# Issuing the transfers of the row maxima from ScalarE instead of the sync queue in a two-layer attention kernel

## The chip, the cores and the metric

One NeuronCore of a Trainium2 chip runs the whole program. The metric is the device time of one execution in microseconds; the program before takes 1774.21 us in the median of three runs. The engines are TensorE (PE, with its weight loads as PEld), VectorE (DVE), ScalarE (ACT), GpSimd (POOL) and the sync engine (SP), which here only issues DMAs.

## The reference

For 8 batches of 512 tokens with 256 channels, two transformer layers are computed. Layer 0 has a causal self-attention and a cross-attention (16 heads of 16 channels each, their outputs added), a projection and a quantized feed-forward net. Layer 1 has a cross-attention and a feed-forward net that is quantized with one scale over all tokens, so its feed-forward runs as a tail when all batches are through. Cut to what matters here:

```python
att = jnp.einsum('bhqd,bhkd->bhqk', q, k) * scale
att = jnp.where(causal[None, None], att, -jnp.inf)
y = jnp.einsum('bhqk,bhkd->bhqd', jax.nn.softmax(att, axis=-1), v)
```

The softmax is what the change touches: the kernel subtracts the maximum of each query's row before it takes the exponential.

## The kernel before, in words

**Units.** An attention unit is `(batch, p, g)`: p is `s` (self-attention of layer 0, causal), `x` (cross-attention of layer 0) or `f` (cross-attention of layer 1), and g one of four groups of four heads. There are 96 units, in the order `ORDER` (line 84). A regular turn of the steady part holds twelve: x0 to x3 and s0 to s3 of one batch and f0 to f3 of the batch before. The text calls them by these names.

**Maxima.** While unit u runs, TensorE also computes the scores of a later unit for their maxima alone (`maxima`, line 1579), and VectorE reduces each bank to a column of negated maxima (line 1372). For the unit after u, POOL then splits the maxima into two float16 parts (`negmax`, line 936, lines 941 to 945), TensorE turns them into rows (`negmax_T`, line 1603, line 1607), ScalarE copies the rows from PSUM to `nrow` (line 1042; the copy itself is line 1007), and two DMAs of 4 KB put them into two more rows of `stack`, next to the queries (line 770, line 774). The final scores of the unit (`scores`, line 1610, line 1619) multiply 50 rows instead of 48, so that the maximum is subtracted within the matmul. The first of them waits for both transfers (line 1615).

**Scores, exponentials, values.** A unit has 16 banks of scores: four blocks j of keys times four heads c. They go through a ring of three PSUM banks: the scores of bank k wait until ScalarE has taken the exponential of bank k-3 (line 1053 is the exponential). Behind the last two heads of a block, TensorE multiplies the probabilities of the block before with the values (`values`, line 1625, line 1633).

**Order.** One list of steps, written out ahead of the run, is walked by every engine, and each takes from it what it has to do (`walk`, line 385). Within a unit (`unit_slot`, line 130), `negmax_T` of the next unit comes after the first two scores of block 2. ScalarE thus does two exponentials of block 2, the copy to `nrow`, whatever other work was dealt to that place, and the other two exponentials. Between them lies the other work of the batch: projections (line 1563, copied by ScalarE at line 1039, split by POOL at 932 and 934, stored by SP at 746), norms, the feed-forward net with its GELU and quantization (ScalarE lines 1075, 1082 and 1088, POOL line 965), and the output projection.

**The sync queue.** SP walks the same list in order and does what it meets: it loads the tokens (734), stores the parts of the projected queries and keys (746), loads them regrouped into `stack` (767, eight DMAs for a unit), stores results (779, 780), and, in `negmax_T`, waits until ScalarE's copy is done and then issues the two transfers. What stands behind such a wait in the list waits too, and `negmax_T` itself stands behind what came before it.

Of the kernel before, what the change touches and what calls it, by code (L numbers as in the profile page):

```python
# [40 lines left out]
NT = T // P  # L41
# [6 lines left out]
PARTS = 2  # L48
ROWS = 3 * D
AUG = ROWS + PARTS  # L50
HALF = P // 2
PAIRS = HU // 2
# [11 lines left out]
STACKS = 4  # L64
# [320 lines left out]
def walk(eng, steps_of):  # L385

    for keys in TURNS:
        for key in keys:
            if key[0] in steps_of:
                steps_of[key[0]](Step(key, None))  # L390
# [4 lines left out]
def two_layers_kernel(nc, x, ctx_512, L0_xattn_Wk, L0_xattn_bk, L0_xattn_Wq, L0_xattn_bq, L0_xattn_Wv, L0_xattn_bv,  # L395
# [4 lines left out]
    with ExitStack() as ctx:  # L400
# [6 lines left out]
        def sem(name):  # L407
            return ctx.enter_context(nc.semaphore(name))
# [16 lines left out]
        def lb(name, shape, dt=F32):  # L425
            return loop.enter_context(nc.sbuf_tensor(name, shape, dt))

        stack = lb("stack", [P, STACKS, 2, PAIRS, T], F16)
# [11 lines left out]
        nrow = lb("nrow", [PARTS * HU * NT, 2, P], F16)  # L440
# [89 lines left out]
        negmax_landed = [sem(f"negmax_landed{i}") for i in range(2)]  # L530
# [61 lines left out]
        def as_f16(tile_):  # L592
            return tile_[:, :].bitcast(F16)
# [19 lines left out]
        def misc_slot(s, k=0, key=None):  # L613
            return s.ring("misc", key).slot(MISC_BANKS, k)
# [5 lines left out]
        def wait_misc_read(eng, s, k=0, key=None):  # L620


            eng.wait_ge(misc_free[misc_slot(s, k, key)], s.ring("misc", key).round(MISC_BANKS, k).at(2))
# [16 lines left out]
        def wait_misc_full(eng, s, k=0):  # L640

            eng.wait_ge(misc_full, s.ring("misc").at(k + 1))
# [42 lines left out]
        def _(sp):  # L685
# [81 lines left out]
                            sp.dma_start(stack[HALF * z + D * row:HALF * z + D * (row + k), r, w, :, :],  # L767
                                         heads_[0:D * k, :, z, :]).then_inc(stack_landed[r], 16)

            def negmax_T(s):  # L770
                r, w = s.n.slot(2), PARTS * PAIRS * NT
                wait_misc_read(sp, s)
                for z in range(2):
                    sp.dma_start(stack[HALF * z + ROWS:HALF * z + AUG, s.n.slot(STACKS), 0, :, :].rearrange("o c (i t) -> o (c i) t", i=NT),
                                 nrow[w * z:w * z + w, r, :]).then_inc(negmax_landed[r], 16)

            def finish(s):
                sp.wait_ge(xn_done["E"], s.b.times(4, 4).at())
                sp.dma_start(batch_of(x_later, s.b.at()), x1_of(s)[:, :, :]).then_inc(stored, 16)
                sp.dma_start(batch_of(xn_later, s.b.at()), xn_of(s, "E")[:, :, :]).then_inc(stored, 16)  # L780

            def finish_most(s):
                if not last_batch(s):
                    finish(s)

            walk(sp, dict(consts_load=consts_load, w_load=w_load, weights=weights, load0=load0, load1=load1, load_mid=load_mid, project=project, settle=settle,
                          stack=stack_, negmax_T=negmax_T, finish=finish_most))


            def tail_free(n):  # L790
# [212 lines left out]
        def _(act):  # L1003
            def copy_misc(s, k, out_, in_=None):
                wait_misc_full(act, s, k)
                slot = misc_slot(s, k)
                act.copy(out_, misc[slot][:, :] if in_ is None else in_(misc[slot])).then_inc(misc_free[slot], 1)
# [34 lines left out]
            def negmax_T(s):  # L1042
                r = s.n.slot(2)
                act.wait_ge(negmax_landed[r], s.n.round(2).times(32, 32).at())
                copy_misc(s, 0, nrow[:, r, :], lambda b: as_f16(b)[0:PARTS * HU * NT, 0:P])

            def scores(s):
                (j, c), n = s.args, s.n
                w = T - P * j if s.unit[1] == "s" else T
                if c == 0:  # L1050
                    act.wait_ge(values_done, n.times(4, VD - P_SLOTS + j + 1).at())
                act.wait_ge(st_full, n.times(16, 4 * j + c + 1).at())
                act.activation(probs[:, j % P_SLOTS, c, T - w:], st_bank(n, 4 * j + c)[:, 0:w], ACT.Exp, scale=scale_of[s.unit[1]]).then_inc(exp_done, 1)  # L1053
# [36 lines left out]
            def down_T(s):  # L1090
                t = s.args[0]
                if t > 1:
                    wait_misc_read(act, s, 0, ("down", s.key[1], t - 2))
                copy_misc(s, 0, hqT[:, t % 2, :, :].rearrange("p k t -> p (k t)"), as_bf16)

            walk(act, dict(consts=consts, consts_rest=consts_rest, bounds=bounds, weights=weights, ctx_T=ctx_T, norm_T=norm_T, project=project, negmax_T=negmax_T, scores=scores,
                           heads_copy=heads_copy, y_T=y_T, quant_T=quant_T, gelu=gelu, hid_peak=hid_peak, down_q=down_q,
                           down_T=down_T))
# [28 lines left out]
        def _(dve):  # L1127
# [247 lines left out]
            def heads_out(s):  # L1375

                _, p, g = s.unit
                slot = misc_slot(s)
                o = misc[slot][:, :].rearrange("p (t c r) -> p t c r", t=NT, c=HU)
                wait_misc_full(dve, s)  # L1380
                dve.reciprocal(rsum[:, s.n.slot(4), :, :], o[:, :, :, D]).then_inc(rsum_done, 1)
                if p == "x" and g == 0:
                    dve.wait_ge(y_summed, s.b.at(1))
                if s.unit == (B - 1, "f", 0):
                    dve.wait_ge(y_summed, B + 1)
                dve.wait_ge(rsum_done, s.n.at(1))
                dve.tensor_tensor(y_of(s, p)[:, :, HU * D * g:HU * D * (g + 1)].rearrange("p t (c d) -> p t c d", d=D),
                                  o[:, :, :, 0:D], rsum[:, s.n.slot(4), :, :].unsqueeze(3).to_broadcast([P, NT, HU, D]),
                                  ALU.mult).then_inc(misc_free[slot], 1)
# [79 lines left out]
        def _(pe):  # L1469
# [155 lines left out]
            def values(s):  # L1625
                j, n, (_, p, g) = s.args[0], s.n, s.unit
                w = T - P * j if p == "s" else T
                if j == 0:
                    pe.wait_ge(v_done[p], s.b.times(2, 2).at())
                    pe.wait_ge(heads_full, n.at(1))  # L1630
                pe.wait_ge(exp_done, n.times(16, 4 * j + 4 + ST_BANKS).at())
                for c in range(HU):
                    last = pe.matmul(acc[32 * c:32 * c + 32, T - w:T], v_of(s, p)[:, j, HU * g + c, :],  # L1633
                                     probs[:, j % P_SLOTS, c, T - w:T], start=j == 0, stop=j == NT - 1)
                last.then_inc(values_done, 1)
# [147 lines left out]
```

## Time and profile before

| | |
|---|---|
| median of 3 runs | 1774.21 us (1771.69 to 1776.6) |
| the profiled execution, its own time | 1775.95 us |
| its span from first to last instruction | 1774.2 us |
| PE, DVE, ACT, POOL busy | 87%, 75%, 64%, 26% of the span |
| mean granted TensorE clock | 0.916 |

The span is 1.75 us shorter than the time of the same execution and agrees with the median within a tenth of a microsecond. In the profile, a row of a timeline gives the start and the length in us of one instruction or a run of equal ones; idle time of the engine ahead of it stands in brackets, with what ended it. SPq is the sync queue's issue of a DMA; its length is the time that the issue held the queue, not that of the transfer.

### The profile page before, as it was taken

Reading aid. Unit: us, or ns where it says so; the run is one execution under the profiler, and the core shown is the slowest. Engines: PE = TensorE matmul, PEld = TensorE weight load, DVE = VectorE, ACT = ScalarE, POOL = GpSimd, SP = SyncE. Lnnn points to the kernel's source line nnn. Section 1 sums busy time; section 2 is a strip of 40 time slices with the busy share of each in tenths; the row PEclk is TensorE's granted clock in tenths of the full one; section 3 lists DMA queues with packets and bytes.
Section 4 is the critical chain, followed back from the end, with each engine's and each line's share of the span. In section 5 each row is a group of like instructions: output and inputs, shape, how many; then the busy total and the mean of one; then the engine's idle time right before and its main releaser. Section 6 shows DMA issues by size and latency. Waiting matters only on the chain.

```text
span 1774.2 us, 31229 instructions
## 1 busy us (share of the span) xinstructions
PE 1550.6 (87%) x11094; PEld 664.0 (37%) x11094; DVE 1325.8 (75%) x2583; ACT 1133.0 (64%) x2178; POOL 464.8 (26%) x677
## 2 busy tenths in 40 slices
PE   3998889988998989988998989998988997888677
PEld 1344335423442334323542335323543442232226
DVE  5787766788678777887687866878578687788287
ACT  1374576566756686666665775667655854866497
POOL 3211413330323122421333122421342222310130
PEclk8788979998999989998998989989998898899898
DMA  6322201212121212121121212121121011011313
GB/s 184 94 83 91 87 19 44 70 45 66 35 76 46 63 43 64 52 76 42 38 77 35 61 43 64 52 75 49 58 64 37 27 55 40 25 56 42 143 60 120
DMA packets 115018, 110.99 MB, mean 63 GB/s; under 512 B 21552, under 2 KB 108720, under 8 KB 114864
## 3 DMA queue, kind: packets, MB, share of 16 engines
q1 hardware_dynamic: 114864, 108.99, 20.6%
q8 instruction: 90, 1.47, 0.3%
q14 instruction: 64, 0.52, 0.1%
HBM read 69.35 MB, written 38.80 MB: 61 GB/s over the span
## 4 chain that ended last, share of the span: by engine, by line
PE 55%; DVE 19%; ACT 13%; issue 5%; POOL 3%; DMA 2%; SPq 2%; ACTq 0%; POOLq 0%; DVEq 0%
PE acc L1633 14%; PE st L1619 10%; DVE nmax L1372 9%; PE misc L1563 8%; PE misc L1535 6%; PE misc L1589 5%; ACT probs L1053 5%; PE misc L1660 3%; PE misc L1575 3%; ACT tail_h L1123 2%; DMA stack<-nrow 2%; PE misc L1600 2%; PE misc L1687 2%; ACT tail_h L1108 1%; DVE hid L1321 1%
## 5 line engine op out<-in xcount | busy, mean ns | idle before, releaser
L1372 DVE TENSOR_REDUCE nmax<-misc 128x1 f32<-128x512 f32 (+3 forms) x1408 | 856.4, 658 | 250.1 <-PE misc L1600 127.3
L1053 ACT ACTIVATE probs<-st 128x512 f32<-128x512 f32 (+3 forms) x1536 | 742.6, 548 | 316.6 <-PE st L1619 213.6
L1619 PE MATMUL st<-stack 50*128 50x512 f16 (+3 forms) x1536 | 458.0, 377 | 68.5 <-ACT probs L1053 54.6
L1589 PE MATMUL misc<-stack 48*128 48x512 f16 (+3 forms) x1536 | 483.2, 377 | 38.6 <-DVE nmax L1372 30.8
L1619 PEld LDWEIGHTS st<-stack 50*128 50x128 f16 x1536 | 110.9, 95 | 460.2 <-ACT probs L1053 263.2
L1633 PE MATMUL acc<-probs,v_x 128*32 128x512 f32 x1152 | 178.5, 696 | 0.0
L1589 PEld LDWEIGHTS misc<-stack 48*128 48x128 f16 x1536 | 125.8, 95 | 110.9 <-DVE nmax L1372 82.2
L1039 ACT ACTIVATE qk<-misc,b 128x512 f32<-128x512 f32 x96 | 65.9, 687 | 149.8 <-PE misc L1563 149.6
L932 POOL TENSOR_TENSOR parts<-qk,zero 128x512 f16<-128x512 f32 x78 | 81.1, 1040 | 297.6 <-ACT qk L1039 297.5
L1633 PE MATMUL acc<-probs,v_s 128*32 128x512 f32 (+3 forms) x1152 | 117.7, 482 | 0.1
L1633 PE MATMUL acc<-probs,v_f 128*32 128x512 f32 x768 | 111.3, 654 | 0.0
L1563 PE MATMUL misc<-xnT_A,W 128*128 128x512 f32 x192 | 101.9, 656 | 0.8 <-DVE nmax L1372 0.8
L941 POOL TENSOR_TENSOR nmax<-nmax,shrink 128x16 f32<-128x16 f32 x96 | 21.6, 225 | 306.5 <-DVE nmax L1372 306.5
L1600 PE MATMUL misc<-mask_mx,identb 64*128 64x128 bf16 (+1 forms) x512 | 98.3, 205 | 0.0
L1600 PE MATMUL misc<-mask_mx_x,identb_x 64*128 64x64 bf16 (+1 forms) x512 | 98.1, 205 | 0.0
L1600 PE MATMUL st<-mask_st,identb 64*128 64x64 bf16 (+1 forms) x512 | 94.1, 205 | 0.0
L1600 PE MATMUL st<-mask_st_x,identb_x 64*128 64x128 bf16 (+1 forms) x512 | 92.0, 205 | 0.0
L934 POOL TENSOR_TENSOR parts<-qk,parts 128x512 f16<-128x512 f32 x78 | 90.2, 1157 | 6.1
L1535 PE MATMUL misc<-ident,heads 128*128 128x128 f32 x384 | 67.5, 302 | 19.3 <-ACT heads L1060 13.4
L965 POOL TENSOR_TENSOR hq<-hid,magic 128x1024 bf16<-128x1024 f32 x32 | 60.6, 1893 | 87.7 <-ACT hid L1088 87.7
L1060 ACT COPY heads<-acc 128x512 f32<-128x512 f32 x96 | 57.2, 596 | 13.6 <-PE acc L1633 11.8
L1535 PEld LDWEIGHTS misc<-ident,heads 128*128 128x128 f32 x384 | 43.5, 149 | 46.5 <-ACT heads L1060 37.8
(282 smaller groups left out, 2090.9 us busy)
## 6 DMA issues: line engine op xcount, KB each, us to landing
parts_xk<-parts SPq DMA_DIRECT2D x36, 128.0 KB
parts_xq<-parts SPq DMA_DIRECT2D x36, 128.0 KB
stack<-parts_xq SPq DMA_DIRECT2D x72, 64.0 KB, 2.1
stack<-parts_xk SPq DMA_DIRECT2D x72, 64.0 KB, 2.1
xn_A<-in_x_dram SPq DMA_DIRECT2D x8, 512.0 KB, 4.3
hid<-in_L_ffn_w_dram SPq DMA_DIRECT2D x4, 1024.0 KB, 5.4
parts_sk<-parts SPq DMA_DIRECT2D x32, 128.0 KB
parts_sq<-parts SPq DMA_DIRECT2D x32, 128.0 KB
```

The lines of the kernel that those rows point to most:

```text
L932: pool.tensor_tensor(parts[:, r, 0, :], qk[:, r, :], zero[:, :].to_broadcast([P, T]), ALU.add).then_inc(qk_split[r], 1)
L934: pool.tensor_tensor(parts[:, r, 1, :], qk[:, r, :], parts[:, r, 0, :], ALU.subtract).then_inc(qk_split[r], 1)
L965: pool.tensor_tensor(hq[:, t % 2, :], hid[:, t, :], magic[:, :].to_broadcast([P, F]), ALU.subtract).then_inc(hq_full, 1)
L1039: act.activation(qk[:, n.slot(QK_RING), :], misc[misc_slot(s)][:, :], ACT.Identity, bias=Bq[w][:, m:m + 1]).then_inc(misc_free[misc_slot(s ...
L1053: act.activation(probs[:, j % P_SLOTS, c, T - w:], st_bank(n, 4 * j + c)[:, 0:w], ACT.Exp, scale=scale_of[s.unit[1]]).then_inc(exp_done, 1)
L1372: dve.tensor_reduce(nmax[:, ring, first:first + NT * (len(cs) - 1) + 1:NT], src, AX.X, ALU.max, negate=True).then_inc(misc_free[slot], 1)
L1535: last = pe.transpose(o[:, P * m:P * m + P], t_, id_[:, :])
L1563: last = pe.matmul(misc[misc_slot(s)][:, :], W[w][:, k, P * m:P * m + P], src[:, k, :], start=k == 0, stop=k == ks - 1)
L1589: last = pe.matmul(o, stack[rows, r, 0, c // 2, P * i:P * i + P], stack[rows, r, 1, c // 2, 0:w], start=True, stop=not causal)
L1600: last = pe.matmul(o[:, parts_[n]], ids[own, :], mask[own, parts_[n]], start=False, stop=n == 1)
L1619: last = pe.matmul(o[:, 0:w], stack[rows, r, 1, c // 2, P * j:P * j + P], stack[rows, r, 0, c // 2, T - w:T], start=True, stop=not causal)
L1633: last = pe.matmul(acc[32 * c:32 * c + 32, T - w:T], v_of(s, p)[:, j, HU * g + c, :], probs[:, j % P_SLOTS, c, T - w:T], start=j == 0, sto ...
```

## The change

The sync engine's step `negmax_T` is taken away. ScalarE's step `negmax_T` keeps its copy and then waits until that copy is done (`wait_misc_read`, the wait that SP had), and issues the same two transfers, which signal the same semaphore as before.

```diff
-            def negmax_T(s):
-                r, w = s.n.slot(2), PARTS * PAIRS * NT
-                wait_misc_read(sp, s)
-                for z in range(2):
-                    sp.dma_start(stack[HALF * z + ROWS:HALF * z + AUG, s.n.slot(STACKS), 0, :, :].rearrange("o c (i t) -> o (c i) t", i=NT),
-                                 nrow[w * z:w * z + w, r, :]).then_inc(negmax_landed[r], 16)
...
                 copy_misc(s, 0, nrow[:, r, :], lambda b: as_f16(b)[0:PARTS * HU * NT, 0:P])
+                wait_misc_read(act, s)
+                w = PARTS * PAIRS * NT
+                for z in range(2):
+                    act.dma_start(stack[HALF * z + ROWS:HALF * z + AUG, s.n.slot(STACKS), 0, :, :].rearrange("o c (i t) -> o (c i) t", i=NT),
+                                  nrow[w * z:w * z + w, r, :]).then_inc(negmax_landed[r], 16)
```

## Rows read from the trace of the kernel before

**Rows 1.** The page: busy time of engines, and the chain by engine.

```profile
PE 1550.6 (87%) x11094; PEld 664.0 (37%) x11094; DVE 1325.8 (75%) x2583; ACT 1133.0 (64%) x2178; POOL 464.8 (26%) x677
PE 55%; DVE 19%; ACT 13%; issue 5%; POOL 3%; DMA 2%; SPq 2%; ACTq 0%; POOLq 0%; DVEq 0%
```

**Rows 2.** Waits of all engines: us in total, times, longest.

```profile
PE st L1619 <- ACT probs L1053: 54.6, 115, 2.5
...
PEld st L1619 <- DMA stack<-nrow: 27.3, 25, 2.7
...
PE st L1619 <- DMA stack<-nrow: 11.8, 12, 2.4
```

**Rows 3.** Timeline of ACT from the copy of s2 on, 690 to 760 us.

```profile
695.14 0.24 ACT L1007 COPY nrow<-misc 32x128 f16<-32x128 f16 x1
...
701.87 1.08 ACT L1053 ACTIVATE probs<-st 128x512 f32<-128x512 f32 x2 [1.23 <-PE st L1600]
```

**Rows 4.** Timeline of SP, 690 to 716 us.

```profile
695.01 1.85 SPq L767 DMA_DIRECT2D stack<-parts_fk  x4
696.90 0.42 SPq L734 DMA_DIRECT2D xmid<-in_x_dram  x1
697.37 1.36 SPq L774 DMA_DIRECT2D stack<-nrow  x2
```

**Rows 5.** Timeline of PE, 699.6 to 701.6 us.

```profile
701.29 0.39 PE L1619 MATMUL st<-stack 50*128 50x512 f16 x1 [1.28 <-DMA stack<-nrow]
```

**Rows 6.** Waits of the sync queue, same columns.

```profile
SPq L774 <- ACT nrow L1007: 280.4, 47, 18.2
```

**Rows 7.** Timeline of ACT at copies of one turn: x0, x3, s0, s1, f1, f2.

```profile
591.23 0.25 ACT L1007 COPY nrow<-misc 32x128 f16<-32x128 f16 x1
591.38 1.07 ACT L1053 ACTIVATE probs<-st 128x512 f32<-128x512 f32 x2
592.75 2.07 ACT L1053 ACTIVATE probs<-st 128x512 f32<-128x512 f32 x4 [0.29 <-PE st L1619]
...
648.66 0.25 ACT L1007 COPY nrow<-misc 32x128 f16<-32x128 f16 x1
648.81 1.24 ACT L1088 ACTIVATE hid<-hid,magic,tok_hq 128x1024 f32<-128x1024 f32 x1
...
664.89 0.24 ACT L1007 COPY nrow<-misc 32x128 f16<-32x128 f16 x1
...
667.41 1.09 ACT L1053 ACTIVATE probs<-st 128x512 f32<-128x512 f32 x2 [0.83 <-PE st L1619]
...
683.01 0.69 ACT L1039 ACTIVATE qk<-misc,b 128x512 f32<-128x512 f32 x1 [1.48 <-PE misc L1563]
...
736.53 1.07 ACT L1007 COPY yT<-misc 128x512 f32<-128x512 f32 x2 [1.03 <-PE misc L1535]
...
753.53 2.07 ACT L1053 ACTIVATE probs<-st 128x512 f32<-128x512 f32 x4 [0.54 <-PE st L1619]
```

**Rows 8.** The tile nrow: duration in ns, min/median/max, first and last start.

```profile
L774 SPq DMA_DIRECT2D stack<-nrow x192: 610/648/1229, 56.4 to 1645.7; - x192
L1007 ACT COPY nrow<-misc x96: 237/243/255, 56.1 to 1644.8; 32x128 f16<-32x128 f16 x96
```

**Rows 9.** One issue line of SP, L767: duration in ns, min/median/max.

```profile
L767 SPq DMA_DIRECT2D stack<-parts_xq x144: 308/425/1480, 34.7 to 1546.0; - x144
```

**Rows 10.** Timeline of SP, 436.5 to 439 us, behind a store of results.

```profile
436.99 1.86 SPq L774 DMA_DIRECT2D stack<-nrow  x2
```

**Rows 11.** Timeline of PE in x0's place, 592.6 to 594 us.

```profile
593.40 0.39 PE L1619 MATMUL st<-stack 50*128 50x512 f16 x1 [0.32 <-ACT probs L1053]
```

**Rows 12.** The chain that ended last, 647 to 653 us.

```profile
648.79 0.12 ACT nrow L1007
648.91 1.14 ACT hid L1088
...
650.19 1.90 POOL hq L965
```

More of the change, by code:

```diff
@@ L786, in _ @@
             walk(sp, dict(consts_load=consts_load, w_load=w_load, weights=weights, load0=load0, load1=load1, load_mid=load_mid, project=project, settle=settle,
-                          stack=stack_, negmax_T=negmax_T, finish=finish_most))
+                          stack=stack_, finish=finish_most))
             def tail_free(n):
```

## The prediction, made before the changed kernel was run

> **What bounds the kernel now.** I read the page first. PE is busy for 87% of the span, DVE for 75%, ACT for 64% [rows 1]. No engine is full, and the chain that ended last says what sets the end: 55% of it is PE, 13% ACT, 5% issue, 19% DVE, and only 2% each DMA and SP's queue [rows 1]. So the kernel runs on TensorE, closely coupled with ScalarE through the three score banks: 115 times a score matmul stood still for an exponential, 54.6 us in all [rows 2].
>
> Then the waits, for what the change aims at. The first scores of a unit wait for the transfers of its maxima. PE itself stood still for them 12 times, 11.8 us together; the weight loads show 27.3 us more in 25 waits, but those lie partly beside matmuls that still ran, so only PE's 11.8 us is lost time [rows 2]. One of the twelve shows how it arises. ScalarE's copy of s2 starts at 695.14 and takes 0.24 us [rows 3], but SP is issuing loads of stack and of xmid until 697.3 and turns to the maxima at 697.37 [rows 4]; PE starts the scores at 701.29 after 1.28 us of idleness [rows 5]. In most units it is the other way round: SP waits for the copy, 280.4 us in 47 waits [rows 6], and the transfer lands while PE still works for the unit before.
>
> Last, ScalarE's own timeline around the copies of one turn, 580 to 775 us [rows 7]. Turns 2 to 5 have nearly the same pattern.
>
> **What goes.** SP loses 192 issues of 0.65 us [rows 8] and the waits for the copy. I price SP's relief itself at nothing: what it issues sooner (stack loads, parts) is not what PE is seen waiting for, and if that cover went it would be bounded by the small DMA share of the chain. The transfers of the twelve late units start as soon as the copy is done. In s2 that is at 695.4 instead of 697.37, 2.0 us earlier, more than the 1.28 us that PE stood still. So I take off all **11.8 us**; the next thing late would be the exponentials of that unit, and ScalarE is idle there, 1.23 us before the first [rows 3].
>
> **What comes.** Each of the 96 copies [rows 8] is followed on ScalarE by a wait for the copy and two issues, with all later exponentials and copies queued behind them. No row shows an issue by ScalarE. The nearest rows are SP's for the very same transfers: a pair holds the queue for 1.36 us [rows 4]. With it goes the overlap that ScalarE has now: the copy at 648.66 ends at 648.91, but the next instruction already starts at 648.81 [rows 7], so 0.1 us; and a few hundredths for the wait's signal. Together **1.5 us** per unit, 144 us of ScalarE's time in all. Bounds: the shortest issue of SP is 0.308 us [rows 9], which makes 0.62 + 0.13 = 0.75 us per unit; a pair behind a large store took 1.86 us [rows 10], which makes 2.0 us. I take 1.5, as it is the same transfer in its usual surroundings.
>
> How much of the 1.5 us reaches PE? ScalarE's next idle time eats into the delay; what is left then meets a PE that waits for banks. Unit by unit of the turn [rows 7]:
> - x0: two exponentials follow the copy, then 0.29 us of idleness. 1.2 us is left, and PE already waits there, 0.32 us for the exponential [rows 11]. Lost: 1.2.
> - x3: right behind the copy comes the scaling of the hidden values (L1088), with no idle time, and it lies on the chain, with POOL's rounding behind it [rows 12]. Lost: 1.5.
> - s0: 0.83 us idle, lost 0.7. f1: 1.03 idle, lost 0.5. f2: 0.54 idle, lost 1.0.
> - the other seven lose nothing: s1 has 1.48 us idle directly behind the copy [rows 7], and x1, s2, s3, f0, f3 are of its kind. In x2 the copy is followed by the squares of the feed-forward net and the score banks are ahead by more than the delay.
>
> That is 4.9 us a turn; 96 units are eight turns' worth, so 39 us. I assume the same rate in the first and the last batches, whose order differs; that is an estimate. Not every late matmul ends late: where the chain runs through DVE, POOL or DMA, PE has room. PE, ACT and issue together hold 73% of the chain [rows 1], so 39 x 0.73 = 28.5 us stays.
>
> **Sum.** 28.5 - 11.8 = +16.7 us. The profiled execution's span of 1774.2 us becomes 1790.9; its own time lies 1.75 us above its span, and the median of the runs, 1774.21, is equal to the span, so the median should come to **1791 us**. At 0.75 us per unit only x0 (0.46), x3 (0.75) and f2 (0.21) lose: 1.4 a turn, 8.3 us after the same share, net -3.5, 1771 us. At 2.0 us the five lose 7.3 a turn and s1 and its kind begin to lose, some 0.8 together: 8.1 a turn, 47 us, net +35.5, 1810 us.
>
> **Rivals.**
> - **Faster: ScalarE's issue is cheap.** If its sequencer takes both issues in some 0.3 us, the delay is 0.4 us; only x3 (0.4) and x0 (0.1) lose, 3 us in all after the share, against 11.8 gained: **1765 us**. It decides below a delay of 0.9 us, where the turn loses about 2 us, 11.5 us in all. For it: no row shows ScalarE issuing. Against it: SP's shortest issue of a stack load took 0.308 us, and these transfers never took less than 0.61 each [rows 8, 9].
> - **No change: the late exponentials are covered.** If PE's other work hides all but x3, which has no cover, 1.5 x 8 = 12 us is paid for 11.8 gained: **1774 us**. For it: DVE has 19% of the chain [rows 1], and the wait for scores that vanishes leaves PE more room. Against it: the stall of PE for the exponential in x0, already there [rows 11].
> - **Slower still: ScalarE and SP get in each other's way.** In the late units SP is in the middle of its own issues when ScalarE would start: until 697.3 in s2 [rows 4]. If each issue of ScalarE then lets one of SP's through (0.42 to 0.68 us in [rows 4]), the delay grows to 2.1 to 2.4 us in s1, s2 and s3 and a little in f0, and they lose about 0.6, 0.85, 0.45 and 0.2: 2.1 a turn, 12 us more after the share, **1803 us**. Nothing in the trace shows two queues issuing at once, since SP alone issues. [...]
>
> **How the numbers follow.** The forecast, 1791 us, gets 0.56, the shared issue 0.15, the cover 0.15 and the cheap issue 0.14. The forecast's own range, by the bounds, is 1771 to 1810. With the near part of the rivals on both sides I give 1767 to 1811: it leaves out the far end of the cheap issue and what lies over a delay of 2 us. A difference of under 0.3%, 5.3 us, is about what a measurement of this kernel can tell from none. Faster by more than that is the cheap issue and the forecast's lowest edge, 0.15; within it the cover and a little of the forecast's lower part, 0.17; slower the rest, 0.68.
>
> **What would show it.** In the changed kernel's profile ScalarE's queue should have 192 issues, in pairs of about 1.35 us, each starting a few hundredths behind its copy, and SP none of them. The wait of the score matmuls for the maxima's transfers should fall from 11.8 us to near nothing, and their wait for exponentials should rise from 54.6 by 20 to 35 us. ScalarE's idle time behind the copies of s1 and its kind should be filled with the issue, at no cost; in x0, x3 and f2 the issue should lie on the chain, with some percent for ScalarE's queue. PE's, DVE's and POOL's busy time should stay. Wrong would be: pairs well under 0.8 us (the cheap issue), pairs over 2 us where SP issues at the same time (the shared one), or pairs of 1.35 us with an unchanged wait for exponentials (the cover).

## The result and the profile after

The changed kernel takes **1802.64 us** (median of 4 runs, 1800.80 to 1804.53) and the kernel before, beside it, 1772.95 us (4 runs, 1769.56 to 1776.60). The ratio is 1.017, with a 95% interval of 1.0146 to 1.0195. The forecast was 1791 us: the sign and the range held, the size did not. +16.7 us was forecast, +29.7 us came.

The profiled execution of the changed kernel took 1800.8 us, its span is 1799.0 us. Line 1617 of the changed kernel is line 1619 of the kernel before, 1631 is 1633, 1561 is 1563, 1533 is 1535, 1086 is 1088, 1051 is 1053, 1032 is 1039, 1000 is 1007, 958 is 965, and 1042 is the new issue on ScalarE. The kernels of the experiments have line numbers of their own.

The page of the changed kernel, beside [rows 1]:

```profile
span 1799.0 us, 31216 instructions
...
PE 1560.0 (87%) x11081; PEld 663.1 (37%) x11094; DVE 1327.1 (74%) x2583; ACT 1134.8 (63%) x2178; POOL 465.8 (26%) x677
...
PE 55%; DVE 17%; ACT 16%; issue 5%; ACTq 3%; POOL 2%; DMA 1%; SPq 0%; POOLq 0%; DVEq 0%
```

More of the chain now lies on ScalarE: ACT went from 13% to 16%, its queue (ACTq) from 0% to 3%; PE keeps its 55%. SP's queue went from 2% to 0%, DMA from 2% to 1%. That is the exchange the change makes: waiting for a late transfer against ScalarE being late. The waits of PE, beside [rows 2], put sizes to it (us in total, times, longest):

```profile
PE st L1617 <- ACT probs L1051: 73.5, 127, 2.6
...
PE st L1617 <- DMA stack<-nrow: 3.6, 2, 1.8
```

The wait for the transfers fell from 11.8 to 3.6 us, the wait for exponentials rose from 54.6 to 73.5 us. The net of the two is +10.7 us, about a third of what was lost; where the rest lies is told further down. The tile nrow, beside [rows 8] (ns, shortest, median, longest; first and last start):

```profile
L1042 ACTq DMA_DIRECT2D stack<-nrow x192: 620/621/1251, 55.1 to 1665.8; - x192
```

So an issue by ScalarE holds its queue for 0.62 us in the median, where SP's took 0.648. Timelines of ScalarE at the copies of x0, x3, s1 and s2, one turn, beside [rows 7] and [rows 3] (start, length; idle time before it in brackets):

```profile
601.22 0.25 ACT L1000 COPY nrow<-misc 32x128 f16<-32x128 f16 x1
601.50 1.27 ACTq L1042 DMA_DIRECT2D stack<-nrow  x2
602.82 3.04 ACT L1051 ACTIVATE probs<-st 128x512 f32<-128x512 f32 x6 [1.35 <-PE st L1617]
606.26 2.07 ACT L1051 ACTIVATE probs<-st 128x512 f32<-128x512 f32 x4 [0.39 <-PE st L1617]
...
659.09 0.24 ACT L1000 COPY nrow<-misc 32x128 f16<-32x128 f16 x1
659.36 1.30 ACTq L1042 DMA_DIRECT2D stack<-nrow  x2
660.71 1.24 ACT L1086 ACTIVATE hid<-hid,magic,tok_hq 128x1024 f32<-128x1024 f32 x1 [1.38 <-issue]
...
695.34 1.27 ACTq L1042 DMA_DIRECT2D stack<-nrow  x2
696.79 0.69 ACT L1032 ACTIVATE qk<-misc,b 128x512 f32<-128x512 f32 x1 [1.48 <-PE misc L1561]
...
709.19 1.30 ACTq L1042 DMA_DIRECT2D stack<-nrow  x2
```

Read them in pairs. In x0 the copy ends at 601.47 and the next exponential starts at 602.82; a pair holds the queue for 1.27 us, with 0.03 ahead of it and 0.05 behind it. With the overlap of 0.1 us that [rows 7] show and that is gone, the delay is **1.45 us** (forecast: 1.5). How much of it is left once the idle time behind it is used up shows in the next group of exponentials. It starts 5.04 us after the copy (606.26 against 601.22), and in the kernel before 3.98 us after it (595.21 against 591.23). So **1.06 us** gets through in this x0, where 1.2 was forecast:

```profile
595.21 2.06 ACT L1053 ACTIVATE probs<-st 128x512 f32<-128x512 f32 x4 [0.39 <-PE st L1619]
```

In s1 the next instruction waits for PE in any case, and its idle time is 1.48 us as in [rows 7]: there the pair is free. In a timeline the idle time in brackets includes the issue, as issues are not counted as busy.

What the delay does to PE and to the chain stands in two views. PE in x0's place, beside [rows 11]:

```profile
603.47 0.39 PE L1617 MATMUL st<-stack 50*128 50x512 f16 x1 [0.84 <-ACT probs L1051]
```

and the chain in x3's place, beside [rows 12]:

```profile
659.22 0.13 ACT nrow L1000
...
659.36 0.65 ACTq L1042
...
660.04 0.62 ACTq L1042
...
660.71 1.25 ACT hid L1086
...
662.10 1.91 POOL hq L958
```

The kernel before went from the copy to the scaling with nothing between them. Now both issues stand between, 1.36 us of them and their gaps, on the chain that ends last.

### The profile page after: what moved, and what is told of

It is laid out like the page before. It is cut to its first block, busy times and chain, and to the rows that moved or that the text cites. A ratio compares the mean times of both kernels' runs of the same rounds, so it can differ in the third digit from the quotient of the medians.

```text
span 1799.0 us, 31216 instructions
## 1 busy us (share of the span) xinstructions
PE 1560.0 (87%) x11081; PEld 663.1 (37%) x11094; DVE 1327.1 (74%) x2583; ACT 1134.8 (63%) x2178; POOL 465.8 (26%) x677
## 4 chain that ended last, share of the span: by engine, by line
PE 55%; DVE 17%; ACT 16%; issue 5%; ACTq 3%; POOL 2%; DMA 1%; SPq 0%; POOLq 0%; DVEq 0%
PE acc L1631 14%; PE st L1617 10%; PE misc L1561 9%; DVE nmax L1370 8%; ACT probs L1051 7%; PE misc L1533 5%; PE misc L1587 5%; PE misc L1658 3%; PE misc L1573 3%; ACTq L1042 3%; ACT tail_h L1121 2%; PE misc L1598 2%; ACT tail_h L1106 1%; PE misc L1685 1%; DVE hid L1319 1%
## 5 line engine op out<-in xcount | busy, mean ns | idle before, releaser
L1617 PE MATMUL st<-stack 50*128 50x512 f16 (+3 forms) x1536 | 470.9, 379 | 81.9 <-ACT probs L1051 73.5
L1587 PE MATMUL misc<-stack 48*128 48x512 f16 (+3 forms) x1536 | 492.4, 377 | 38.5 <-DVE nmax L1370 30.8
L925 POOL TENSOR_TENSOR parts<-qk,zero 128x512 f16<-128x512 f32 x78 | 81.3, 1042 | 295.3 <-ACT qk L1032 295.2
L1658 PE MATMUL misc<-W,yT 128*128 128x256 f32 x256 | 59.5, 385 | 0.8 <-ACT yT L1000 0.8
```

The costliest lines, as they stand in the source:

```text
L925: pool.tensor_tensor(parts[:, r, 0, :], qk[:, r, :], zero[:, :].to_broadcast([P, T]), ALU.add).then_inc(qk_split[r], 1)
L1587: last = pe.matmul(o, stack[rows, r, 0, c // 2, P * i:P * i + P], stack[rows, r, 1, c // 2, 0:w], start=True, stop=not causal)
L1617: last = pe.matmul(o[:, 0:w], stack[rows, r, 1, c // 2, P * j:P * j + P], stack[rows, r, 0, c // 2, T - w:T], start=True, stop=not causal)
L1658: last = pe.matmul(misc[misc_slot(s, h)][:, C * t:C * t + C], yT[:, m, first:first + P], W[k + "o"][:, m, :], start=m == 0, stop=m == KC - 1)
```

## The experiments

The theory to be tested is the prediction's: a fixed delay on ScalarE that costs in the places without idle time behind the copy, against a gain in twelve late units. Its rivals are that the two queues hold each other up (then s1, s2, s3 and f0 pay), that SP's running ahead costs, and that the wait and not the issue is dear.

Twelve kernels ran, in four groups, each group beside its own runs of the kernel before. The table has all of them. The last two columns need a word: single executions of the kernel before lie between 1762.37 us (mean granted TensorE clock 0.928) and 1783.48 us (0.909), and over 73 of them the time goes with the clock, 10 us less for 0.01 more (correlation -0.89, 2.2 us of scatter about the line). "Off the line" is how far a kernel's executions lie, in the mean, above that line at their own clock. It takes out what goes with the clock, whichever way the cause runs; for e8 and a part of e5 the line is drawn out beyond its ends. It is a way to sort the numbers and no measurement by itself: the four groups of the kernel before lie between 0.8 us under the line and 1.3 us above it in the mean, so a difference of 2 us off the line says little.

| kernel | median us (runs) | before, us | ratio, 95% interval | mean clock | off the line, us |
|---|---|---|---|---|---|
| the change | 1802.64 (4) | 1772.95 | 1.0170 (1.0146 to 1.0195) | 0.9125 | +22 |
| e9, the change again | 1801.56 (6) | 1771.92 | 1.0158 (1.0123 to 1.0193) | 0.914 | +23 |
| e1, ACT issues in the 12 late units | 1761.05 (6) | 1772.88 | 0.9929 (0.9903 to 0.9955) | 0.923 | -9 |
| e10, in s1, s2, s3, f0 | 1761.07 (9) | 1771.92 | 0.9935 (0.9911 to 0.9958) | 0.922 | -10 |
| e11, in x1, x2 | 1776.70 (12) | 1771.92 | 1.0024 (1.0001 to 1.0046) | 0.921 | +4.5 |
| e3, in x1, x2, s1, s2, s3, f0 | 1779.14 (12) | 1772.88 | 1.0031 (1.0004 to 1.0057) | 0.915 | -1.5 |
| e12, in x3 | 1787.31 (8) | 1776.25 | 1.0077 (1.0049 to 1.0104) | 0.915 | +9 |
| e2, in x0, x3, s0, f1, f2, f3 | 1808.34 (6) | 1772.88 | 1.0200 (1.0171 to 1.0229) | 0.915 | +31 |
| e4, SP as before, ACT issues two others | 1794.31 (6) | 1772.88 | 1.0130 (1.0101 to 1.0158) | 0.916 | +17 |
| e6, only the wait on ACT | 1773.07 (12) | 1770.23 | 1.0005 (0.9981 to 1.0028) | 0.921 | +1 |
| e7, one transfer each | 1782.25 (12) | 1770.23 | 1.0054 (1.0030 to 1.0079) | 0.918 | +7 |
| e5, the change, SP keeps its wait | 1809.10 (6) | 1770.23 | 1.0201 (1.0164 to 1.0237) | 0.911 | +27 |
| e8, POOL issues | 1839.53 (6) | 1770.23 | 1.0386 (1.0350 to 1.0422) | 0.900 | +48 |

### Which units pay: e1, e2, e3

The kernels e1, e2, e3, e10, e11 and e12 split the change by unit. They differ in one line, the set in which ScalarE waits for the copy and issues both transfers; in the other units SP does it, as before.

```diff
+        def act_issues(u):
+            b, p, g = u
+            return (p == "s" and g >= 2 and 1 <= b <= 5) or u in ((7, "x", 0), (5, "f", 0))   # e1
+            return (p, g) in (("x", 0), ("x", 3), ("s", 0), ("f", 1), ("f", 2), ("f", 3))     # e2
+            return (p, g) not in (("x", 0), ("x", 3), ("s", 0), ("f", 1), ("f", 2), ("f", 3)) # e3
+            return (p, g) in (("s", 1), ("s", 2), ("s", 3), ("f", 0))                         # e10
+            return (p, g) in (("x", 1), ("x", 2))                                             # e11
+            return (p, g) == ("x", 3)                                                         # e12
...
+                if act_issues(s.unit):
+                    return
...
+                if not act_issues(s.unit):
+                    return
```

e1 takes the twelve units for whose transfers PE stood still (s2 and s3 of batches 1 to 5, x0 of batch 7, f0 of batch 5). Expected:

> ScalarE issues the pair only in the twelve units whose first scores stood still for the transfers before (s2 and s3 of batches 1 to 5, x0 of batch 7, f0 of batch 5); SP issues the other 84 as before. Theory A (ScalarE's seat: the pair blocks ScalarE for 1.4 us, which costs where ScalarE has no idle time behind the copy, and nothing where it has): the 11.8 us of waits go, nothing is paid, 10 us faster than before, about 1763 us. Theory B (every issue on ScalarE costs about the same, some 0.4 us a unit): 11.8 gained against 5 paid, about 1766. Theory C (what costs is SP's order of transfers, not ScalarE): about 1763 as A, since SP keeps its place in 84 units.

It is 0.7% faster. The tile nrow and the waits of e1 show that it does what it says:

```profile
L780 SPq DMA_DIRECT2D stack<-nrow x168: 610/648/1224, 56.5 to 1632.5; - x168
...
L1057 ACTq DMA_DIRECT2D stack<-nrow x24: 620/622/1258, 309.6 to 1441.6; - x24
```

```profile
PEld st L1632 <- DMA stack<-nrow: 11.1, 13, 1.0
...
PE st L1632 <- DMA stack<-nrow: 0.2, 1, 0.2
```

The wait of the weight loads is down from 27.3 us and PE's own from 11.8 us [rows 2]. So the gain of the change is real, 9 to 12 us, and it comes from those twelve units.

e2 takes the units that the prediction charged, with f3 beside them, where starts of units had slipped in the changed kernel although no loss was forecast. Expected:

> ScalarE issues in x0, x3, s0, f1, f2 and f3 only (48 units), SP elsewhere. Theory A: all of the loss and none of the gain, 30 to 40 us slower than before, 1803 to 1813 us. Theory B: half of the loss, some 20 us slower, about 1793. Theory C: SP still waits in half of the units, some 10 to 15 us slower, about 1786.

48 units, half of the change, cost more than the whole: +35.5 us by the medians. There is no gain in it: PE still stands 13.1 us for late transfers, as in [rows 2], as s2 and s3 are left to SP. Of the other half, e3, a gain was expected:

> ScalarE issues in x1, x2, s1, s2, s3 and f0 only (48 units), SP elsewhere. Theory A: all of the gain and little of the loss, 5 to 10 us faster than before, 1763 to 1768 us. Theory B: half of the loss against all of the gain, 8 us slower, about 1781. Theory C: some 5 us slower, about 1778.

That missed. The median is 0.3% above, and its twelve executions fall apart: three took 1764 to 1767 us at a clock of 0.921 to 0.923, nine took 1773 to 1784 us at 0.909 to 0.915. At its own clock e3 gains 1.5 us, which is within the scatter. Its profile is of one of the three fast executions and shows the gain, as PE stands only 1.6 us for late transfers.

### Is x1 or x2 to blame for that: e10, e11, and x3 by itself: e12

> ScalarE issues in s1, s2, s3 and f0 only (32 units), SP elsewhere: the kernel with the 48 idle units without x1 and x2. If the pair costs nothing where ScalarE is idle behind the copy, and the loss of the 48 came from x1 and x2 (whose copies stand among the steps of the feed-forward net): 8 to 12 us faster than before, 1760 to 1765 us. If there is a price per issue wherever it stands: a third of the cost of the change against all of the gain, as before or a few us slower, 1772 to 1778.

> ScalarE issues in x1 and x2 only (16 units). If x1 and x2 cost: 10 to 18 us slower than before, 1782 to 1790 us. By a price per issue: a sixth of the cost, 5 to 7 us slower, 1778. By the working of the prediction (both hidden): no change.

> ScalarE issues in x3 only (8 units), SP elsewhere. Behind x3's copy stands the scaling of the hidden values, which the prediction put on the chain with no cover: 8 times 1.45 us, 10 to 14 us slower than before, 1782 to 1786 us. If that scaling is covered after all: no change. By a price per issue: a twelfth of the cost, 3 us slower, 1775.

e10 is as fast as e1, with 32 units instead of 12. It holds eleven of e1's twelve units. So in s1, s2, s3 and f0 ScalarE's issue costs nothing that shows here, as [rows 7] said of s1's idle time. e11 costs a little (its interval reaches from 0.01% to 0.46%), where the prediction had none. By itself that would suit a price per issue, 5 to 7 us; e10 and e12 rule such a price out. By the medians e10 and e11 come to -11 + 5, and e3, which is both together, measured +6; off the line it is -10 + 4.5 = -5 against -1.5, within what such runs leave uncertain. So most of e3's miss goes with its lower clock. What makes the clock fall in e3 and not in e10 is not settled.

One thing that adds to x2 can be seen. Where a pair comes right behind SP's store of results, it takes ScalarE 1.85 us instead of 1.27, in two of e11's sixteen pairs. Timeline of SP, then of ScalarE, in e11:

```profile
440.48 0.43 SPq L786 DMA_DIRECT2D xn_later<-xn_C  x1
...
441.11 1.85 ACTq L1057 DMA_DIRECT2D stack<-nrow  x2
```

SP's issue of the store is over when the pair starts. In the prediction's long pair [rows 10] SP was alone, behind its own store; here a pair in the other queue is lengthened behind it as well.

e12 prices the one unit of the turn to which the prediction gave no cover at all. Eight pairs of 1.45 us are 11.6 us; measured are +11.1 us by the medians and +9 off the line.

### The cost by itself: e4, e6, e7

In e4 SP keeps both transfers; ScalarE waits for its copy all the same and issues two transfers of 4 KB that nobody needs, so nothing is gained and only the delay is paid.

```diff
                 copy_misc(s, 0, nrow[:, r, :], lambda b: as_f16(b)[0:PARTS * HU * NT, 0:P])
+                wait_misc_read(act, s)
+                for z in range(2):
+                    act.dma_start(spare[s.n.at(), z], ident[16 * z:16 * z + 16, 0:P // 2].bitcast(F16)).then_inc(spared, 16)
```

> SP issues all transfers as before; behind each copy ScalarE waits for it and issues two transfers of 4 KB of a constant to DRAM that nobody needs. Theory A: the cost without the gain, 30 plus 12 us and less what the tail's loads do, 35 to 42 us slower than before, 1808 to 1815 us. Theory B: the same. Theory C: no change of SP's order, so within 10 us of before, up to 1783.

It cost 21 us, about half of what was expected. The tile spare shows a reason:

```profile
L1051 ACTq DMA_DIRECT2D spare<-ident x192: 308/405/1724, 55.8 to 1652.9; - x192
```

These issues took 0.405 us in the median and not 0.62, though the transfers are as large, so the dummy was a poor copy. With 2 x 0.405 + 0.13 = 0.94 us of delay, the prediction's own idle times leave 0.65 (x0), 0.95 (x3), 0.1 (s0) and 0.4 (f2), 2.1 a turn, 17 us in all ahead of any cover and some 13 behind the cover that e12 shows (9 of 11.6). Off the line e4 measured 17, so 4 us of it are not accounted for. 13 of the 192 issues took 0.72 to 1.72 us and may be a part of it. 12 of the 13 ran beside an issue of SP's, but so did 176 of the 192.

In e6 ScalarE only waits for its copy and SP issues as before (first diff); in e7 ScalarE issues the second of the two transfers and SP the first (second diff).

```diff
                 copy_misc(s, 0, nrow[:, r, :], lambda b: as_f16(b)[0:PARTS * HU * NT, 0:P])
+                wait_misc_read(act, s)
```

```diff
                 wait_misc_read(sp, s)
-                for z in range(2):
+                for z in range(1):
...
                 copy_misc(s, 0, nrow[:, r, :], lambda b: as_f16(b)[0:PARTS * HU * NT, 0:P])
+                wait_misc_read(act, s)
+                w = PARTS * PAIRS * NT
+                for z in (1,):
...
```

> The kernel before, with ScalarE waiting for its own copy behind it, and SP issuing as before. Theory A: only the lost overlap of about 0.15 us a unit, in the struck units, at most 4 us slower, 1773 to 1777 us. A rival, by which the wait and not the issue is what costs: 15 us or more slower, 1788 and up.

> ScalarE issues the second transfer of each pair, SP the first as before. Theory A: the delay is 0.75 to 0.8 us instead of 1.4; of it x0 0.5, x3 0.8, f2 0.25 and f3 some, about 13 us in all are lost, and the late units gain nothing or little: 10 to 15 us slower than before, 1783 to 1788. Theory B (a price per issue): half of the cost alone, 20 us slower, 1793.

The wait is free (+0.05%, interval -0.19% to +0.28%). One issue costs +0.5%, less than half of two, and with hardly any gain beside it, since the other transfer is as late as before: PE still stood 9.9 us for transfers in 6 places. The time, 1782.25 us, lies just under the 1783 to 1788 expected. What idle time swallows (0.29 us in x0, 0.83 in s0 [rows 7]) is taken off the first part of a delay.

e7 is also the sharpest test of the rival by which the two queues hold each other up, the shared issue, as both queues turn to the same unit within 0.02 us of each other in 52 of the 96 units. Timeline of SP, then of ScalarE, in one such unit, and the tile nrow of e7:

```profile
612.04 0.65 SPq L774 DMA_DIRECT2D stack<-nrow  x1
...
612.04 0.62 ACTq L1049 DMA_DIRECT2D stack<-nrow  x1
```

```profile
L774 SPq DMA_DIRECT2D stack<-nrow x96: 616/663/850, 55.8 to 1652.8; - x96
L1049 ACTq DMA_DIRECT2D stack<-nrow x96: 620/621/1546, 55.8 to 1652.8; - x96
```

If one had to wait for the whole of the other, one of them would hold its queue for about 1.25 us (0.62 + 0.65). In those 52 units SP's issues took 0.62 to 0.75 us and ScalarE's 0.62 to 0.65, with one exception: ScalarE's first issue of the run, 1.55 us. That one says little, as ScalarE's first issue of this transfer is long in every kernel, beside SP or not (1.24 us in e12, where SP issued nothing at that time). Nor does a wait show behind the issue: in x3's place, where the next work is ready, ScalarE's issue starts at 658.62 with SP's, takes 0.62 us, and the scaling starts at 659.29, 0.05 us behind it. A wait of a tenth of a microsecond can't be excluded.

### SP's running ahead: e5

Freed of its waits [rows 6], SP does all its later work sooner. e5 takes that away: SP still waits for the copy, but issues nothing. Against the changed kernel, shortened:

```diff
+            def negmax_T(s):
+                wait_misc_read(sp, s)
...
```

> The changed kernel, but SP still waits at its old place in the list for ScalarE's copy, without issuing anything, so its other transfers keep nearly the order and time of before. Theory A (ScalarE's seat alone): as the changed kernel, 1800 to 1804 us. Theory C (part of the loss comes from SP running ahead: in the last three units the bulk loads of the tail then lie in front of the maxima's transfer, which took over 4 us): 4 to 9 us faster than the changed kernel, 1794 to 1798 us.

Both expectations missed. e5 takes 1809.10 us, 38.9 us more than the kernel before beside it, where the change takes 29.7 and e9 29.6 us more; off the line it is 4 to 5 us slower than the change. So SP's running ahead is not where the time went; on the whole it seems to be worth some microseconds. A part of it is seen at the start, where PE's wait for the first transfers is 3.3 us long in e5 and 1.8 in the changed kernel. The rest isn't traced. In the tail, running ahead does cost something. Timeline of SP in the changed kernel:

```profile
1645.92 0.32 SPq L803 DMA_DIRECT2D w1T<-w1T_later  x1
...
1648.93 0.39 SPq L791 DMA_DIRECT2D ctx_C<-xn_later  x1
```

These are the first and the last of seven loads, in the middle of the last units. ScalarE's pair for f2 of the last batch comes behind them, at 1652.07:

```profile
1652.07 1.27 ACTq L1042 DMA_DIRECT2D stack<-nrow  x2
```

and PE has to wait for it:

```profile
1658.24 0.60 PE L1617 MATMUL st<-stack 50*128 50x512 f16 x3 [1.83 <-DMA stack<-nrow]
```

In the kernel before, SP's pairs of those units stood in front of the loads in its one queue:

```profile
1634.98 11.38 SPq L774 DMA_DIRECT2D stack<-nrow  x4
1646.54 0.33 SPq L810 DMA_DIRECT2D w1T<-w1T_later  x1
```

(The row of 11.38 us is two pairs, 10 us apart.) The 1.83 us are half of the 3.6 us that the wait for the transfers still has. In e5, where SP waits and the loads come later, PE stands only 0.4 us for a transfer there.

### Another engine: e8

POOL is busy for 26% [rows 1], so it looked like the place for the issues. Against the changed kernel, shortened:

```diff
+            def negmax_T(s):
+                r, w = s.n.slot(2), PARTS * PAIRS * NT
+                wait_misc_read(pool, s)
+                for z in range(2):
...
```

> POOL issues both transfers behind a wait for ScalarE's copy; SP and ScalarE do not. Theory A: ScalarE pays nothing, the late units gain; POOL is idle for three quarters of the time and its splits of the projections have room: 0 to 10 us faster than before, 1763 to 1773 us, if POOL's own issue takes up to 2 us; where its transfers land 1 us later than SP's, the gain of the late units is gone and it is as before. Theory C (SP running ahead costs): as the changed kernel without ScalarE's part, some 5 us slower than before, 1778.

That missed by 70 us. The waits of e8:

```profile
POOL stack L943 <- ACT nrow L1006: 345.4, 64, 18.0
...
PE st L1619 <- DMA stack<-nrow: 14.7, 7, 5.2
```

POOL walks its list in order as well, and stands 345 us in front of a copy that ScalarE hasn't made yet, with its splits, its rounding and the next maxima behind it. SP had the same wait, 280 us [rows 6], but with nothing of the sort behind it. That is the likely cause; no run parts POOL's waits from its 192 issues, which hold its queue for 0.602 us each in the median. POOL's free share of 74% said nothing about whether it could afford to wait at this place.

### The change once more, at the same count of records: e9

The profile of the changed kernel lacks 13 matmul records (11081 against 11094). e9 is the same kernel again.

> The changed kernel once more, beside the two below, to bring it into the same runs. Whatever the theory: 1798 to 1806 us; over 1806 would say that the kernel in which SP keeps its wait is no slower than the change itself.

It repeats the result, +29.6 us. Its page:

```profile
span 1802.3 us, 31229 instructions
...
PE 1566.0 (87%) x11094; PEld 664.4 (37%) x11094; DVE 1327.9 (74%) x2583; ACT 1134.9 (63%) x2178; POOL 465.9 (26%) x677
```

and the page of e10, with the same count:

```profile
span 1761.4 us, 31229 instructions
...
PE 1541.9 (88%) x11094; PEld 663.7 (38%) x11094; DVE 1325.6 (75%) x2583; ACT 1134.9 (64%) x2178; POOL 465.8 (26%) x677
```

Span less busy time is what PE stood idle. Before [rows 1]: 1774.2 - 1550.6 = 223.6 us. e9: 236.3, so **+12.7 us of stalls**. e10: 219.5, -4.1 us. But PE's busy time, with the same matmuls, went up by **15.4 us** in e9 and down by 8.7 in e10. ACT, DVE and POOL agree within 2.1 us.

How the clock comes in can be seen in one place, f3, where PE did not stand for ScalarE. Timeline of PE before:

```profile
768.41 1.42 PE L1633 MATMUL acc<-probs,v_f 128*32 128x512 f32 x8
769.77 3.28 PE L1563 MATMUL misc<-xnT_A,W 128*128 128x512 f32 x4
```

and after:

```profile
781.72 1.93 PE L1631 MATMUL acc<-probs,v_f 128*32 128x512 f32 x8
783.59 3.74 PE L1561 MATMUL misc<-xnT_A,W 128*128 128x512 f32 x4
```

The same twelve matmuls take 0.97 us longer. Here are the stretches ahead of and around them, PE's busy time third and its granted clock behind the five engines, as a share of full speed, first before:

```profile
761.00:765.00 4.00, 2.73 (x20) 0.74 (x19) 3.83 (x13) 1.86 (x4) 0.42 (x2) 1.00 0.39 114
765.00:768.40 3.40, 1.66 (x9) 0.39 (x5) 3.37 (x7) 2.20 (x5) 0.00 (x0) 1.00 0.20 59
768.40:773.00 4.60, 4.60 (x15) 1.36 (x16) 1.43 (x3) 0.34 (x1) 0.00 (x0) 0.63 0.01 2
```

then after:

```profile
774.00:778.00 4.00, 2.80 (x16) 0.78 (x16) 3.83 (x13) 2.12 (x5) 0.44 (x2) 0.86 0.39 112
778.00:781.70 3.70, 3.14 (x13) 0.56 (x9) 3.67 (x9) 1.34 (x3) 0.00 (x0) 0.50 0.20 56
781.70:787.20 5.50, 5.50 (x13) 1.38 (x12) 1.22 (x3) 1.09 (x2) 0.00 (x0) 0.51 0.01 1
```

PE is busy for 68% and 49% of the first two stretches before, and for 70% of the first one after. Cut into slices of 0.5 us, the kernel before shows a clock of 0.99 to 1.00 or of 0.50 to 0.51 in all but 61 of 3548. In this place it is 0.50 before only in the third row and for a part of it, from 769.0 to about 772, and after already from 777.0, in the first row, and until the twelve matmuls are nearly done, at about 787. Over the whole span, with these two levels, the stretches at 0.50 add up to 2 x (1 - 0.916) x 1774.2 = 298 us before and 2 x (1 - 0.913) x 1802.3 = 314 us in e9; e10, at 0.923, has 271. At 1.00 eight value matmuls and four projections of the same shapes took 1.06 and 1.98 us (744.60 and 745.59 before), at 0.50 the 1.93 and 3.74 us above, and a score matmul for the maxima, of 512 columns, took 0.39 us (768.10 before) and 0.60 us (780.59 after). So PE did at least half of the work in a stretch at 0.50, and by this estimate 16 us more of it is worth at most 8 us of the 15.4; the other 7 I can't place. Each of these profiles is a single execution, and that of the kernel before had a lower clock, 0.916, than the mean of its executions, 0.921.

## Why the prediction was right, and where it was wrong

**The delay held.** 1.5 us was forecast for a pair with its wait and its lost overlap, 1.45 is what it takes. The nearest row, SP's pair [rows 4], was the right price to take. With it fall the cheap issue, which needed under 0.9 us, and, as e2 costs three times what e12 does, the covered one, which asked that only x3 pays. PE's wait for exponentials rose by 18.9 us (16.8 in e9), just under the 20 to 35 us that were to show it.

**The places held, as far as they were tested.** x3 pays 9 to 11 us for its eight pairs (e12), s1, s2, s3 and f0 pay nothing (e10), and 1.06 us gets through in one x0 (forecast: 1.2). Charged with nothing and yet paying were x1 and x2, some 5 us together if e11's median is taken, and perhaps f3, whose 0.97 us in one turn go with the clock. No run moves x0, s0, f1, f2 or f3 by itself: e2 without e12's share leaves 22 us for the five together, where 20 were forecast for four of them.

**The loss, after its cover: 28.5 forecast, about 31.** The prediction's 39 us are what it added up from the delays; e2, which has these places and f3 and no gain, measured +31 off the line, so 0.80 of the sum reached the end and not 0.73. For x3 alone it is 9 of 11.6, nearly the same share. That is a small miss. The prediction's reason for the share, the make-up of the chain, was not tested.

**The gain: 11.8 forecast, 8 to 10.** What failed here is "I price SP's relief itself at nothing". In the steady part the waits are gone as forecast, and in s2 PE now starts the scores without idle time:

```profile
712.65 1.15 PE L1533 MATMUL misc<-ident,xn_A 128*128 128x128 f32 x8
713.73 0.39 PE L1617 MATMUL st<-stack 50*128 50x512 f16 x1
```

But the relief put the tail's loads in front of the last transfers. In the changed kernel 11.8 - 3.6 = 8.2 us of the gain was kept. (The other 1.8 us of waiting is at the start of the kernel.) By e5 the relief as a whole was worth something all the same: with SP held at its old waits the kernel was slower still, by 4 to 9 us. A smaller slip of the reading is that SP waits for the copy "in most units"; 47 of 96 [rows 6] is just under half.

**The step that failed, and the larger: "PE's, DVE's and POOL's busy time should stay".** For DVE and POOL it is so, for PE it is not, and the working took every matmul at its length of before. 31 - 9 is +22 us, which is what the change and e9 measured off the line (+22 and +23). That it agrees so closely is luck in part. It leaves out the 4.5 us of x1 and x2, and the two halves of the change, e2 and e3, come to 31 - 1.5 = +30 off the line and to +42 by their medians; so the parts do not simply add up: 4 to 8 us off the line, and 12 by the medians, stay open. The rest from 22 up to 29.7, **some 8 us**, goes with the granted clock, which is 0.913 in the changed kernel and 0.921 in the mean of 73 executions before. In the same way e1 and e10 gain 11 to 12 us by their medians and 9 to 10 off the line, at a clock of 0.922 to 0.923. That the delays bring the clock down is one reading, as the slowest kernels have the lowest clock (e8 0.900, e5 0.911). But e12 with 8 pairs has the same clock as e2 with 48 (0.915), so their number does not set it. No run changed the clock by itself: it is a correlation, and the cause of these 8 us is not shown.

**The shared issue.** This rival's number, 1803 us, was met, and its mechanism wasn't. In s2's place of the changed kernel SP's queue runs

```profile
708.78 1.90 SPq L767 DMA_DIRECT2D stack<-parts_fk  x4
```

at the same time as ScalarE's pair at 709.19 above. SP's four took 1.85 us when it issued alone [rows 4], ScalarE's two took 1.30, as against 1.27 in x0. The rival had 2.1 to 2.4 us. In e7 two issues that start together take at most 0.1 us more than SP's alone, but for ScalarE's first, and e10, with the units that were to pay, pays nothing. That each issue of ScalarE lets one of SP's through was the author's assumption; no run here shows it for these transfers beyond that tenth of a microsecond. The pair behind the store in e11, 1.85 us instead of 1.27, suggests that the queues are not wholly independent, but such pairs are too few to make 12 us: four of the 96 in the changed kernel took over 1.4 us, the longest, the first of the run, 1.91. A total that comes out right is no evidence for its mechanism.

## What to carry to other kernels

In this kernel a DMA issue on a compute engine cost most of its length (0.62 us) where work stood right behind it, and nothing that shows where the engine would have been idle; so decide it place by place, from the idle time behind each place in that engine's timeline, and not for the whole step. Here ScalarE issues in s1, s2, s3 and f0 and SP in the rest, and the kernel takes 1761.07 us, 0.65% less than before (interval 0.42% to 0.89%) and 2.2% less than the change beside it (e9); e1, with 12 units alone, does the same. And where, as here, PE is busy for 87% of the span, add to the forecast what goes with the granted clock, for which the spread of the kernel's own executions is a measure: here 1762 to 1783 us, at 0.930 to 0.909.

## What the hardware showed that was not expected

- The time of one and the same kernel varied between 1762 and 1783 us with its mean granted clock between 0.930 and 0.909. A net of a few microseconds can be doubled or wiped out by it, as in e3.
- ScalarE's issues of two 4 KB transfers of the same size took 0.62 us (nrow to stack) and 0.405 us (ident to memory), in the median. Issues of the first kind took POOL 0.602 us (e8) and SP 0.648 us: here the kind of transfer mattered more (0.215 us on ScalarE) than which engine issued it (0.046 us at most).
- ScalarE's first issue of nrow to stack took 1.24 to 1.33 us wherever it stood in the run (at 55 us in the change, 135 us in e10, 310 us in e1), and 1.55 us in e7. The following ones took 0.62 to 0.64 us in the median. Why the first is long is not known.
- Two queues that issued the same kind of transfer at the same time did not take turns: but for the first issue, 0.62 to 0.65 us beside 0.62 to 0.75 us in e7, where SP alone takes 0.648 [rows 8]. A pair of ScalarE's right behind SP's store of results took 1.85 us instead of 1.27 (e11).
